# Flamingo block on one core: the last attention heads projected ahead of a feed-forward, the first combinations at a step's end, zeros and low halves placed elsewhere

## The reference

```
x = x + tanh(g_xattn[0]) * L0_xattn(ctx, layernorm(x), mask)   # 8 heads of 64
x = x + tanh(g_ffn[0])   * L0_ffn(layernorm(x))                # 8 experts, two per token (sparse mixer)
x = x + tanh(g_xattn[1]) * L1_xattn(ctx, layernorm(x), mask)   # 16 heads of 64
x = x + tanh(g_ffn[1])   * L1_ffn(x)                           # quantised rows and weights, conv of 3 taps, silu
```

## Time and profile before

| | |
|---|---|
| runs, us | 1513.42, 1514.56, 1524.12; median 1514.56 |
| profiled execution, us | 1526.41, its span 1524.7 |
| mean granted TensorE clock | 0.949 of full speed |
| busy, share of the span | PE 83%, DVE 70%, ACT 64%, POOL 71% |
| instructions | PE 16920, DVE 2854, ACT 2319, POOL 1347 |

### The profile page before, as it was taken

How to read it: one execution, slowest core, us unless ns; L and a number is a source line. 1 busy time by engine, 2 the same in 40 slices (tenths; PEclk the granted TensorE clock), 3 DMA queues, 4 the chain that set the end, 5 groups by cost and what they waited for, 6 DMA issues and landing times.

```text
span 1524.7 us, 45219 instructions
## 1 busy us (share of the span) xinstructions
PE 1269.2 (83%) x16920; PEld 986.9 (65%) x16920; DVE 1059.9 (70%) x2854; ACT 980.7 (64%) x2319; POOL 1085.8 (71%) x1347
## 2 busy tenths in 40 slices
PE   2877878779988868778999999899999999998853
PEld 1555656557777756556888887666666676766642
DVE  5867878856555657776666666777787777777654
ACT  3968877655555646555656566677777777777731
POOL 5877877786766644465767676788788888887752
PEclk9989989899999989989999999999999999999975
DMA  7699988579999868369999997444444554445310
GB/s 232 126 195 244 211 179 205 130 201 230 247 222 254 197 151 164 70 131 228 234 262 237 267 230 185 76 96 103 98 97 91 100 95 105 94 92 91 77 40 7
DMA packets 444859, 239.97 MB, mean 157 GB/s; under 512 B 389361, under 2 KB 424033, under 8 KB 436833
## 3 DMA queue, kind: packets, MB, share of 16 engines
q1 hardware_dynamic: 412152, 178.51, 56.9%
q10 hardware_dynamic: 29416, 51.22, 11.1%
q0 software_dynamic: 3072, 7.34, 1.7%
HBM read 107.78 MB, written 35.50 MB: 94 GB/s over the span
## 4 chain that ended last, share of the span: by engine, by line
PE 36%; ACT 15%; DVE 12%; DMA 10%; issue 9%; POOL 8%; SPq 5%; DVEq 3%; ACTq 2%; POOLq 0%
PE bank_ring L1135 7%; DMA expert_up<-experts_up 6%; PE bank_ring L1173 5%; PE bank_ring L1121 5%; DVE scores L1402 5%; PE bank_out L1154 4%; ACT scores L891 4%; PE bank_x L1236 4%; ACT probs L898 3%; PE bank_scores L1095 3%; ACT values L918 3%; POOL probs L686 3%; PE bank_x L1187 2%; SPq L551 2%; PE bank_x L1108 2%
## 5 line engine op out<-in xcount | busy, mean ns | idle before, releaser
L686 POOL TENSOR_TENSOR probs<-scores,probs 112x487 f16<-112x487 f32 x378 | 419.7, 1128 | 220.7 <-ACT probs L898 217.6
L891 ACT ACTIVATE scores<-scores,score_min 112x487 f32<-112x487 f32 x384 | 265.8, 693 | 119.7 <-DVE score_min L1402 116.7
L1424 DVE SCALAR_TENSOR_TENSOR values<-bank_ring,values 128x512 f16<-128x512 f32 x192 | 132.3, 689 | 219.3 <-ACT values L918 215.5
L1402 DVE CUSTOM_DVE_ANT_0 scores<-bank_scores,mask 112x487 f32<-112x487 f32 x384 | 238.0, 657 | 2.8 <-PE bank_scores L1095 2.3
L898 ACT ACTIVATE probs<-scores 112x487 f16<-112x487 f32 x384 | 213.8, 604 | 25.0 <-DMA probs_turned<-probs 9.0
L918 ACT ACTIVATE values<-bank_ring 128x512 f16<-128x512 f32 x192 | 113.1, 589 | 134.1 <-PE bank_out L1154 132.0
L1135 PE MATMUL bank_ring<-weights,kv_B 128*128 128x128 f16 x3072 | 196.2, 221 | 1.4 <-DVE keys L1419 1.4
L1154 PE MATMUL bank_out<-values,probs_turned 128*128 128x64 f16 x4608 | 172.9, 196 | 23.8 <-issue 16.5
L1135 PEld LDWEIGHTS bank_ring<-weights,kv_B 128*128 128x128 f16 x3072 | 185.0, 99 | 10.4 <-DVE keys L1419 2.1
L1121 PE MATMUL bank_ring<-kv_B,weights 128*128 128x488 f16 x768 | 182.2, 374 | 0.0
L1154 PEld LDWEIGHTS bank_out<-values,probs_turned 128*128 128x128 f16 x4608 | 161.1, 100 | 27.5 <-issue 25.2
(11 more groups left out here) (237 smaller groups left out, 2416.5 us busy)
## 6 DMA issues: line engine op xcount, KB each, us to landing
expert_up<-experts_up SPq DMA_DIRECT2D x43, 1024.0 KB, 5.6
expert_down<-experts_down SPq DMA_DIRECT2D x43, 512.0 KB, 6.6
raw_weights<-in_weights ACTq DMA_DIRECT2D x8, 1536.0 KB, 10.9
experts_up<-expert_up ACTq DMA_DIRECT2D x8, 1024.0 KB, 6.1
probs_turned<-probs SPq DMA_TRANSPOSE x384
context_turned_B<-kv_B ACTq DMA_DIRECT2D x16, 375.0 KB, 7.8
kv_B<-context_turned_B ACTq DMA_DIRECT2D x16, 375.0 KB, 3.9
moe_results<-moe_result SPq DMA_DIRECT2D x43, 128.0 KB, 4.5
```

Source lines behind the costliest of these rows:

```text
L686: pool.tensor_tensor(PR[:, u % 4, 1, 0:KEYS], S[:, u % 4, 0:KEYS], PR[:, u % 4, 0, 0:KEYS], ALU.subtract).then_inc(probs_split[u % 2], 1)
L891: act_e.activation(S[:, u % 4, 0:KEYS], S[:, u % 4, 0:KEYS], ACT.Exp, bias=rmin[:, u % 4:u % 4 + 1], scale=-1.0, accum_out=rsum[:, g % 2, ...
L1402: dve.tensor_tensor_reduce(out=S[:, u % 4, 0:KEYS], in0=bS[u % 2][0:TOK, 0:KEYS], in1=mask[:, m, 0:KEYS], scale=1.0, scalar=3.0e38, op0=AL ...
L1424: dve.scalar_tensor_tensor(vN[:, j % 2, 1].rearrange("p t d -> p (t d)"), bank("v", j)[:], 1 / WSCALE, vN[:, j % 2, 0].rearrange("p t d -> ...
```

## The change

It consists of five edits. (1) The last group of heads has no slack any more, so its `norm_out`, `o_turn` and `o_proj` come one step sooner, and the steps of sequence 14's feed-forward from `tanh0` on are pushed behind it, its `f_rate` to the early tasks; sequence 15 gets a table of its own, `F_LAST`. (2) Both halves' side taps of sequence 14 go to GpSimd, and there the side taps of sequences 14 and of 15's half 0 stand behind the step's low halves instead of ahead of them; only half 1 of sequence 15 stays on VectorE, now behind the tasks of its step. (3) The first combinations of both batches, with the `stats("B", n)` that follow, stand at the end of VectorE's step. (4) The zeros of the first batch go out in six pieces at step 0 instead of nine pieces in steps 1 to 17, those of the second batch from step 61 instead of 57. (5) VectorE takes the second head's low half in the first batch's scatter steps too, 33 to 37.

```diff
-ZERO_TILES, ZERO_FROM = (2, 3), (1, 57)
+ZERO_TILES, ZERO_FROM = (3, 3), 61
 def slack(g):
-    return 0 if g in (BATCHES[0][1] - 1, BATCHES[1][1] - 1) else 1
+    return 0 if g in (BATCHES[0][1] - 1, BATCHES[1][1] - 1, PAIRS // 4 - 1) else 1
-           "sides1": 15, "tanh0": 15, "tanh1": 16, "act0": 16, "act1": 16, "max0": 16, "max1": 17, "rate": 17,
-           "scale0": 18, "scale1": 18, "down": 20, "store": 21}
+           "sides1": 15, "tanh0": 17, "tanh1": 19, "act0": 18, "act1": 20, "max0": 19, "max1": 20, "rate": 21,
+           "scale0": 21, "scale1": 22, "down": 23, "store": 24}
+F_LAST = {"stats": 11, "rstd": 11, "rows": 12, "round": 12, "turn": 12, "up0": 13, "up1": 13, "sides0": 14,
+          "sides1": 14, "tanh0": 14, "tanh1": 15, "act0": 15, "act1": 15, "max0": 15, "max1": 16, "rate": 16,
+          "scale0": 17, "scale1": 17, "down": 18, "store": 19}
-VECTOR_SPLITS = range(routed(1) + 3, first_tile_step(1))
+VECTOR_SPLITS = [range(routed(b) + 3, first_tile_step(b)) for b in range(2)]
 # sync engine
+                if j == 0:
+                    sp.wait_ge(zeros_set, 1)
+                    for k in range(len(ZERO_PIECES[0])):
+                        zero_rows(0, *ZERO_PIECES[0][k])
+                if 0 <= j - ZERO_FROM < len(ZERO_PIECES[1]):
+                    zero_rows(1, *ZERO_PIECES[1][j - ZERO_FROM])
 # gpsimd, in a step
-                        if not on_vector(n, i) and j == f_step(n, f"sides{i}"):
+                        if n < NSEQ - 2 and j == f_step(n, f"sides{i}"):
                             conv_sides(n, i)
...
+                for n, i in ((NSEQ - 2, 0), (NSEQ - 2, 1), (NSEQ - 1, 0)):
+                    if j == f_step(n, f"sides{i}"):
+                        conv_sides(n, i)
 # vector engine, in a step
-                    if j == combine_step(n):
-                        combine(n)
-                    if j == start_b(n) - 6:
-                        stats("B", n)
+                    if n not in (BATCHES[0][0], BATCHES[1][0]):
+                        if j == combine_step(n):
+                            combine(n)
+                        if j == start_b(n) - 6:
+                            stats("B", n)
...
+                for n in (BATCHES[0][0], BATCHES[1][0]):
+                    if j == combine_step(n):
+                        combine(n)
+                        stats("B", n)
+                if j == f_step(NSEQ - 1, "sides1"):
+                    conv_sides(NSEQ - 1, 1)
```

More of the change, by code:

```diff
@@ L142, in f_step @@
 def f_step(n, name):
-    return start_b(n) + (F_QUICK if n >= NSEQ - 2 else F_MIDDLE if n == NSEQ - 3 else F_STEPS)[name]
+    steps = {NSEQ - 1: F_LAST, NSEQ - 2: F_QUICK, NSEQ - 3: F_MIDDLE}
+    return start_b(n) + steps.get(n, F_STEPS)[name]
 def p_step(n, first, at):
@@ L557, in _ @@
                     sp.dma_start(X[:, 6:NSEQ], x_in[6:NSEQ].rearrange("n t d -> t n d")).then_inc(x_loaded[3], 16)
-                for b in range(2):
-                    k, rest = divmod(j - ZERO_FROM[b], 2 - b)
-                    if rest == 0 and 0 <= k < len(ZERO_PIECES[b]):
-                        zero_rows(b, *ZERO_PIECES[b][k])
+                if j == 0:
[4 more added lines that the diff above has]
+                    zero_rows(1, *ZERO_PIECES[1][j - ZERO_FROM])
                 if (j - 3) % 4 == 0 and 0 < (j + 5) // 4 < NSEQ:
@@ L726, in conv_sides @@
                 if n or j:
-                    pool.wait_ge(conv_done, 2 * n + j - (1 if n == NSEQ - 1 else 0))
+                    pool.wait_ge(conv_done, 2 * n + j)
                 for tap in (1, 2):
@@ L797, in _ @@
                     split_hidden(m[1], m[2], m[3])
-                if is_pair(j) and j not in VECTOR_SPLITS:
-                    if j == VECTOR_SPLITS[-1] + 1:
+                if is_pair(j) and not any(j in steps for steps in VECTOR_SPLITS):
+                    if any(j == steps[-1] + 1 for steps in VECTOR_SPLITS):
                         pool.wait_ge(turned[(2 * j - 1) % PT_BUFS], turns_done(2 * j - 1))
                     split_probs(2 * j + 1)
+                for n, i in ((NSEQ - 2, 0), (NSEQ - 2, 1), (NSEQ - 1, 0)):
+                    if j == f_step(n, f"sides{i}"):
+                        conv_sides(n, i)
                 for b in range(2):
@@ L998, in conv_tanh @@
             def conv_tanh(n, j):
-                if on_vector(n, j):
-                    act_e.wait_ge(conv_last, n - NSEQ + 3)
+                if (n, j) == (NSEQ - 1, 1):
+                    act_e.wait_ge(conv_last, 1)
                 else:
-                    act_e.wait_ge(conv_done, 2 * n + j + (0 if n == NSEQ - 1 else 1))
+                    act_e.wait_ge(conv_done, 2 * n + j + 1)
                 act_e.activation(hpads[j][:, :, 1:TOK + 1], hacts[n % 2][:, 4 * j:4 * j + 4, :], ACT.Tanh, scale=0.5)\
@@ L1751, in _ @@
                 for n in range(NSEQ):
-                    if j == combine_step(n):
-                        combine(n)
-                    if j == start_b(n) - 6:
-                        stats("B", n)
+                    if n not in (BATCHES[0][0], BATCHES[1][0]):
[3 more added lines that the diff above has]
+                            stats("B", n)
                     if j == start_b(n) - 5:
                         b_apply(n)
-                    if j == f_step(n, "stats"):
+                    if n < NSEQ - 1 and j == f_step(n, "stats"):
                         stats("F", n)
@@ L1763, in _ @@
                         f_round_rows(n)
-                    if on_vector(n, 1) and j == f_step(n, "sides1"):
-                        conv_sides(n, 1)
                     for i in range(2):
@@ L1777, in _ @@
                     gate_hidden(m[0][1], m[0][2], m[0][3])
-                if j == ZERO_FROM[1]:
+                if j == ZERO_FROM:
                     dve.memset(zero_row, 0.0).then_inc(row_zeroed, 1)
@@ L1781, in _ @@
                     part(t)
+                if j == f_step(NSEQ - 1, "stats"):
+                    stats("F", NSEQ - 1)
                 for n in range(NSEQ):
@@ L1798, in _ @@
                         norm_out(g)
-                if is_pair(j) and j in VECTOR_SPLITS:
-                    if j == VECTOR_SPLITS[0]:
+                if is_pair(j) and any(j in steps for steps in VECTOR_SPLITS):
+                    if any(j == steps[0] for steps in VECTOR_SPLITS):
                         dve.wait_ge(turned[(2 * j - 1) % PT_BUFS], turns_done(2 * j - 1))
```

2 lines of the change are left out of this document (1 added, 1 removed).

## The result

The changed kernel takes 1511.48 us, the median of 20 runs (1506.61 to 1521.21). The kernel before, run 20 times in turn with it, takes 1524.72 us (1513.42 to 1533.34). The ratio is 0.9927 with a 95% interval of 0.9908 to 0.9947: 0.73% faster, or 8 to 14 us of 1524.72. (The quotient of the two medians is 0.9913; they lie 13.2 us apart.) In the ratios here, a run more than 1.5% above the fastest of its kernel is left out. The forecast was 1500, from 1489 to 1511. The way was right, the gain by the ratio, 11 us, is three quarters of the 14.4 to 15.9 us that were summed up, and the time lies half a microsecond above the range.

A forecast was written before the change was run, and what follows sets the result against it. TensorE, busy 83% of the span, was taken as the bound, so only shortening its waits counts. Terms 7.6 + 5.5 + 2.2 + 0.6 = 15.9 us; less the landing's 1.5, 14.4 off the median 1514.56 gave 1500, range 1489 to 1511.

The forecast's parts named there:

- The sum's last step: Whole kernel: 15.9 us off the profiled 1526.41 gives 1510.5; without the landing's 1.5, 14.4 off the median 1514.56 gives 1500.
- The tail: End of the program, new order and side taps on GpSimd: 7.6 us earlier, with bounds of 5 and 10.
- steps 1 to 5: End of the program: sequence 13's `f_down` 4.85 us earlier, sequence 15's statistics 10.7 earlier, its side taps 8.8 earlier.
- Step 6: End of the program: sequence 14's `f_down` add behind both `f_act` delays `f_max`, 1.24 us lost, leaving 7.6.
- step 5: Sequence 15's statistics to VectorE's side taps: these come at 1495.2, 8.8 us earlier; GpSimd's second set costs nothing.
- The first combinations: Steps 58 and 106, scores no longer queued behind the second gather's wait: 5.5 us gained, between 3 and 11.
- The order's 2.05: Step 58: scores 1.9 us after the gather's landing instead of 3.95, with four operations done during the wait; 2.05 us.
- The term for the landing: Step 58: second gather lands sooner with the zeros moved to step 61; 1.5 us taken of a possible 5.6.
- The low halves: Step 37's mask wait: four halves off GpSimd give 2.2 us, between 0 and 4.4.
- loss of 0.38 for each half: GpSimd's scatters before step 37's mask: an issue beside a VectorE half takes 1.33 us instead of 0.95.
- other waits take over: Whole kernel: step 37's and the combinations' gains pass to other waits, tail only 5; about 1507.5 us; chance 0.25.
- the 0.6: Steps 1 to 17: first batch's zeros gone from there, one piece's transfer saved, 0.6 us.

The follow-up runs named there:

- run 20: Not a label but a count: the kernel before, run 20 times in turn with the changed kernel, takes 1524.72 us.
- the side taps alone: Side taps of sequence 14 and of 15's half 0 on GpSimd behind its low halves, old tables, on the kernel before: ratio 1.0016 (0.9990–1.0043).
- Z S: Both batches' zeros moved and VectorE's low halves in steps 33 to 37 added, nothing else, on the kernel before: ratio 1.0017 (0.9986–1.0047).
- C S: First combinations at the end of VectorE's step and its low halves in steps 33 to 37, on the kernel before: ratio 0.9992 (0.9960–1.0024).

## Why the prediction was wrong where it was

- **The sum's last step failed, the choice of a base.** The prediction had 1510.5 us from the profiled execution (1526.41 − 15.9) and took 1500 from the median of three runs, holding the 11.85 us between them to be perhaps the shortened stalls. Over 20 runs the median before is 1524.72; two of the three runs shown are the lowest of the 20. 1524.72 − 14.4 would have been 1510.3, against 1511.48. Of the 11.5 us by which the forecast is too low, 10.2 are this step.
- **The tail**: 7.6 forecast, 7.8 in the trace after, where the granted clock was like that of the trace before; up to 10.2 in kernels with both edits and the full clock there, which the prediction didn't consider. The marks of steps 1 to 5 lie 0.8 to 1.8 us earlier than worked out. Step 6 came as worked out, 1.2 lost; the longer side taps (4.73 instead of 4.20) stood in no step, and why they are longer is open. The sentence in step 5 that GpSimd's second set costs nothing is right only with edit 1, as the side taps alone show.
- **The first combinations**: 5.5 forecast, 7.2 in the stages of the traces (5.0 in steps 57 to 60, 2.2 in 105 to 108, averages of the table). The order's 2.05 measured 2.01 to the scores, 2.2 over the stage. The term for the landing was mis-sized: 1.5, and the second batch's zeros are worth 2.7.
- **The low halves**: 2.2 forecast, 0. First, the prediction's condition "if GpSimd never pauses there" failed: 2.1 of the 4.3 us became a wait for ScalarE. Its loss of 0.38 for each half was misread: the issue of 1.33 us is the longest of six in the second batch that ran beside a half for over 0.2 us (0.94 to 1.33), and issues beside none took up to 1.24; measured it is 0.3 to 0.7 us for all twelve issues. Second, that the mask is followed at once by a wait for the first tile's rows, and that one by the third tile's weights, was not counted. The rival "other waits take over" holds here. The Trainium skill's rule that the two engines share interfaces ("GPSIMD Engine Reference", Key points) would have given GpSimd 1.8 us. The traces' 1.3 to 2.0 agree with that number by luck, since the wait for ScalarE makes most of the difference.
- **The zeros**: no cost at step 0, as forecast; the 0.6 can't be told from the spread of that stage.
- **What stays open.** The stages' terms add up to 7.8 + 7.2 = 15 us, the timed gain is 8 to 14. That the sum came so near is partly luck: 2.2 and 0.6 that were not there stand against 1.7 too little for the combinations. Edits 1 and 2 without the others were not run, so the 7.2 us are not timed by themselves; Z S and C S, which hold parts of them, time as the kernel before (1.0017 and 0.9992). Edit 5 may cost some of the difference: the five kernels with edits 1 to 3 and without edit 5 have ratios of 0.9873 to 0.9925, the four with it 0.9915 to 0.9948. The intervals overlap, and no stage of the traces holds a loss, so this is not shown.

## What to carry to other kernels

Before a gain is subtracted, ask how much of the spread of the runs the base may be: three runs that differ by 11 us fix no base for a forecast of 15, and the profiled execution, whose own stalls the sum was made from, was the better one here; it is one draw too, and happened to lie 1.7 us above the median of the 20. Before work is credited as time gained on an engine, ask what the engine will then be early for: GpSimd gave up 4.3 us of work and came at most 2.0 us sooner. A shortened wait is worth only what lies between it and the next resource on the same engine's list; where a chain runs into transfers, list the next two or three arrivals before crediting anything. Two edits on one ring can be worth little alone (here −1.0 and 3.4 us) and more together (7.8): judge a move of work to another engine together with the order of the work that reads it.

## What the runs showed that was not expected

Executions of one kernel differ by 12 to 29 us (19.9 for the 20 of the kernel before). In the traces of all kernels the difference stands in steps 0 to 33 (233 to 244 us), 40 to 57 (178 to 186) and 64 to 105 (357 to 366), while steps 108 to 184 agree within 1.7 us (446.9 to 448.6). The DMA engines' mean busy share is 0.78 or more in the former and 0.48 to 0.49 in the latter. The granted clock differs too: 0.91 to 0.94 in steps 0 to 33 and 0.95 to 0.98 in 64 to 105, but 1.00 in 108 to 184. Of the 20 runs of the kernel after, the five longest (1516.99 to 1521.21) have a mean clock of 0.947 to 0.950, the others 0.950 to 0.958. Whether transfers make TensorE wait and the clock falls for it, or the clock comes first, no run separates.

With a context load of 375 KB issued within 1 us of it, the transpose of 128 rows kept TensorE waiting until 6.1 to 9.5 us after its issue, in the five traces where TensorE waited; with that load a step later 3.9 us were enough.
